# Attention's first two maxima and exponentials ahead of the projection's last rotation

## The reference

```python
q = (x @ Wq + bq).reshape(B, T, H, HD)
k = (x @ Wk + bk).reshape(B, T, HKV, HD)
q, k = _rope(q, cos, sin), _rope(k, cos, sin)
scores = jnp.einsum('bgjtd,bjsd->bgjts', q, k) * scale
scores = jnp.where(mask[None, None, None], scores, -jnp.inf)
wei = jax.nn.softmax(scores, axis=-1)
out = jnp.einsum('bgjts,bjsd->bgjtd', wei, v)
```

## Time and profile before

| what | value |
|---|---|
| time, median of 3 runs | 2125.2 us (2123.72 to 2127.41) |
| the profiled execution: its time | 2124.0 us |
| its span in the trace | 2122.2 us |
| PE busy | 2057.8 us (97% of the span) |
| DVE busy | 1718.2 us (81%) |
| ACT busy | 1370.4 us (65%) |
| mean granted clock of TensorE | 0.989 |

### The profile page before, as it was taken

The page is one execution under the profiler, slowest core; times in us unless marked ns, Lnnn a source line. Parts: engine busy times, 40 slices in busy tenths (PEclk is TensorE's granted clock), DMA queues, the critical chain, the costliest instruction groups (busy, mean ns, idle before and its releaser), DMA issues.

```text
span 2122.2 us, 39177 instructions
## 1 busy us (share of the span) xinstructions
PE 2057.8 (97%) x13409; PEld 1827.4 (86%) x13409; DVE 1718.2 (81%) x3648; ACT 1370.4 (65%) x2752; POOL 851.1 (40%) x818
## 2 busy tenths in 40 slices
PE   8999989999999999999999999999959999999998
PEld 6888878999889998899988999888748999999996
DVE  5899987888678877788767887678877898988887
ACT  3677776766667666676666766433326777777774
POOL 1000013333233332333323333144455777788774
PEclk9999999999999999999999999999979999999999
DMA  7557553110331104311053110567637999999998
GB/s 250 189 213 277 218 213 125 70 60 21 130 120 71 61 21 138 111 70 60 21 203 107 69 62 19 193 239 287 238 122 201 299 298 298 298 297 293 301 287 258
DMA packets 139633, 361.25 MB, mean 170 GB/s; under 512 B 16336, under 2 KB 33232, under 8 KB 134864
## 3 DMA queue, kind: packets, MB, share of 16 engines
q1 hardware_dynamic: 111376, 292.03, 39.2%
q0 software_dynamic: 28096, 67.12, 13.2%
HBM read 224.21 MB, written 134.89 MB: 169 GB/s over the span
## 4 chain that ended last, share of the span: by engine, by line
PE 75%; DVE 5%; ACT 2%; issue 2%; DMA 1%; POOL 0%; DVEq 0%; POOLq 0%; ACTq 0%
PE p_S L665 18%; PE p_O L700 17%; PE p_TP L677 11%; PE p_pgu L1453 9%; PE p_acc L1050 4%; PE p_prest L1453 4%; PE p_py L1470 4%; PE p_tp L1439 3%; PE p_py L1471 1%; PE p_py L1472 1%; DVE p_hi_hot L1237 1%; ACT p_prob L744 1%; DMA o_scratch<-p_oT 1%; ACT p_pT1h L753 0%; PE p_picked L1483 0%
## 5 line engine op out<-in xcount | busy, mean ns | idle before, releaser
L665 PE MATMUL p_S<-p_kT,p_q 128*128 128x512 f32 (+3 forms) x1920 | 474.0, 377 | 12.5 <-ACT p_prob L744 12.0
L665 PEld LDWEIGHTS p_S<-p_kT,p_q 128*128 128x128 f32 x1920 | 323.8, 190 | 63.3 <-ACT p_prob L744 19.2
L859 POOL TENSOR_SCALAR p_prob<-p_prob,p_inv 128x128 f32<-128x128 f32 (+7 forms) x256 | 191.3, 747 | 452.3 <-DVE p_inv L808 452.3
L859 POOL TENSOR_SCALAR p_prob<-p_prob,p_inv,p_part 128x1024 f32<-128x1024 f32 x128 | 153.0, 1195 | 483.4 <-DVE p_inv L813 483.4
L677 PE MATMUL p_TP<-p_ident,p_prob 128*128 128x128 f32 x2176 | 303.5, 274 | 2.4 <-DVE p_pT1l L819 2.1
L677 PEld LDWEIGHTS p_TP<-p_ident,p_prob 128*128 128x128 f32 x2176 | 244.4, 141 | 30.7 <-issue 17.9
L797 DVE TENSOR_REDUCE p_nmax<-p_S 128x1 f32<-128x1024 f32 (+7 forms) x256 | 253.1, 989 | 20.8 <-PE p_S L665 15.5
L753 ACT CAST p_pT0h<-p_TP 128x512 fp32r<-128x512 f32 (+3 forms) x320 | 155.0, 527 | 135.0 <-PE p_TP L677 134.4
L753 ACT CAST p_pT1h<-p_TP 128x512 fp32r<-128x512 f32 (+3 forms) x320 | 154.8, 526 | 128.8 <-PE p_TP L677 128.2
L1723 POOL DMA_INDIRECT sum_scratch<-p_y,p_tokT x124 | 206.0, 1661 | 42.6 <-issue 37.2
L700 PE MATMUL p_O<-p_pT0h,p_v 128*128 128x256 f32 x1088 | 222.8, 288 | 0.0
(11 more groups left out here) (284 smaller groups left out, 4635.0 us busy)
## 6 DMA issues: line engine op xcount, KB each, us to landing
p_w_raw<-in_gu SPq DMA_DIRECT2D x64, 768.0 KB, 6.9
qk_scratch<-p_qout SPq DMA_DIRECT2D x80, 512.0 KB, 2.8
p_q<-qk_scratch SPq DMA_DIRECT2D x16, 2048.0 KB, 9.0
o_scratch<-p_oT SPq DMA_DIRECT2D x128, 256.0 KB, 2.1
p_ot<-o_scratch SPq DMA_DIRECT2D x32, 1024.0 KB, 7.4
p_w_raw<-in_gu SPq DMA_DIRECT2D x64, 256.0 KB, 8.3
v_scratch<-p_vout SPq DMA_DIRECT2D x16, 512.0 KB, 3.2
p_t_raw<-in_dn SPq DMA_DIRECT2D x32, 256.0 KB, 8.2
```

Source lines behind the costliest of these rows:

```text
L665: mm = nc.tensor.matmul(out, x, y, start=(n == 0), stop=(n == 2))
L859: nc.gpsimd.tensor_scalar(prob[k][:, cols], prob[k][:, cols], inv[:, k:k + 1], scale, ALU.mult, ALU.mult).then_inc(normed, 1)
```

## The change

Before the last rotation of the projection, DVE takes the maxima of attention's units 0 and 1, and ACT, right after the swap of block 79, their exponentials. DVE then does rotate(79) and join(79) and enters attend; the low halves of blocks 77, 78 and 79 follow one each at the end of attention's steps 2, 3 and 4. ACT makes the high parts of blocks 77 to 79 after the two exponentials. No instruction is added or taken away; PE, POOL and SP have the programs that they had, and SP's stores of blocks 77 to 79 wait for the same counts.

```diff
-        def scalar(act):
+        def scalar(act, first_exps):
...
                         swap(q, n, k, t, first and k == 0 and t < 2)
+                        if last and k == 1 and t == NT - 1:
+                            first_exps(act)
                         if t >= 2:
                             q_hi_part(q - 2, k, t - 2, i, first)
...
-        def vector(dve):
+        def vector(dve, first_maxima):
...
                     for t in range(NT):
+                        if last and k == 1 and t == NT - 1:
+                            first_maxima(dve)
                         rotate(n * NT + t, n, k, t, first and k == 0)
+                        if last and k == 1 and t == NT - 1:
+                            join(n * NT + t, t, False)
+                            return
                         if t >= 2:
                             q_lo_part(n * NT + (t - 2), k, t - 2)
...
-            for t in (NT - 2, NT - 1):
-                q_lo_part(NH * NT - NT + t, 1, t)
+            return [lambda dve, t=t: q_lo_part(NH * NT - NT + t, 1, t) for t in range(1, NT)]
...
-        FREE = 2
+        FREE, AHEAD = 2, 2
...
-        def steps(eng, step, tail, between={}):
+        def steps(eng, step, tail, between={}, early={}):
             for j in range(HKV):
                 for i in range(U):
                     step(j, i, j == 0)
+                    for piece in early.get((j, i), []):
+                        piece(eng)
...
+            if first_only:
+                for u in range(AHEAD):
+                    exp(0, u, 0)
+                return
...
-                    if i < U and a < ngrp(i):
+                    if i < U and a < ngrp(i) and not (first and i < AHEAD):
                         exp(j, i, a)
...
+            if first_only:
+                for u in range(AHEAD):
+                    row_max(0, u, 0)
+                return
...
-                if i < U:
+                if i < U and not (first and i < AHEAD):
                     row_max(j, i, 0)
...
+                  {(0, AHEAD + n): [piece] for n, piece in enumerate(rest)})
...
-            project.scalar(act)
+            project.scalar(act, lambda act: attend.scalar(act, None, first_only=True))
             attend.scalar(act, early[0])
...
-            project.vector(dve)
-            attend.vector(dve, early[1])
+            rest = project.vector(dve, lambda dve: attend.vector(dve, None, first_only=True))
+            attend.vector(dve, early[1], rest)
```

More of the change, by code:

```diff
@@ L731, in tensor, with scalar @@
             pe.wait_ge(exped, HKV * SG[U])
-        def scalar(act, between):
-            act.sem_inc(weighed, FREE)
+        def scalar(act, between, first_only=False):
+            if not first_only:
+                act.sem_inc(weighed, FREE)
             def exp(j, u, a):
@@ L769, in step, with vector @@
                         p_hi(*args)
-                    if i < U and a < ngrp(i):
+                    if i < U and a < ngrp(i) and not (first and i < AHEAD):
                         exp(j, i, a)
             steps(act, step, OUT - 2, {U + 1: between[0:1], U + 2: between[1:2], U + 3: between[2:4]})
-        def vector(dve, between):
-            dve.sem_inc(turn_lo, FREE)
-            dve.sem_inc(o_lo, FREE)
+        def vector(dve, between, rest=(), first_only=False):
+            if not first_only:
+                dve.sem_inc(turn_lo, FREE)
+                dve.sem_inc(o_lo, FREE)
             def take_k(j):
@@ L847, in step @@
                     p_lo(*args)
-            steps(dve, step, OUT - 2, {U + 2: between[0:1], U + 3: between[1:2], U + 4: between[2:3], OUT - 2 + U: between[3:4]})
+            steps(dve, step, OUT - 2, {U + 2: between[0:1], U + 3: between[1:2], U + 4: between[2:3], OUT - 2 + U: between[3:4]},
+                  {(0, AHEAD + n): [piece] for n, piece in enumerate(rest)})
         def gpsimd(pool):
```

## The result

| what | before | changed |
|---|---|---|
| median, 13 runs each | 2125.2 us (2123.39 to 2128.66) | 2131.22 us (2129.93 to 2135.81) |
| ratio to before | | 1.0028, 95% interval 1.0021 to 1.0035 |
| span of the profiled execution | 2122.2 us | 2128.1 us |

The change makes the kernel 6.0 us slower, by 0.28%; the interval of the ratio is 4.5 to 7.4 us. The forecast was 2128.6, in the right direction, with too small a size; the range ended at 2130.4, 0.8 us short.

What follows compares the result with a forecast made beforehand. The border was taken as bound by low half 79, its store, the load of queries and pair 0's landing behind it. Landing +1.4 and half clock +2.0 us on 2124.0, plus 1.2 to the median, gave 2128.6 us; range 2121.8 to 2130.4.

Steps and rivals of the forecast that it cites:

- What bounds the border: Projection to attention: low half 79, its store, load of queries, pair 0's store landing, then unit 13's scores set the time.
- Maxima and exponentials first: Behind unit 1's scores: PE's gap shrinks from 5.36 to about 1.2 us, 4.2 us earlier for PE alone.
- The low halves' sum: DVE's attend steps up to low half 79 sum to 2.95 us; it ends at 294.9, bounds 294.5 to 295.8.
- The load: SP's load of queries goes out at 297.8, 1.4 us later than before; bounds +1.0 to +2.7.
- it then lands the same 9.7 us after the load's issue: Pair 0's output store, queued behind the load of queries, lands at 307.5, with 1 us allowed either way.
- The range: For the whole kernel's time: 2121.8 to 2130.4 us, with some 0.1 of chance left out on either side.
- the case's own range: The forecast case alone, landing plus clock: 2125.2 + 0 to 2125.2 + 5.6 us; the case had chance 0.46.
- rival 3: Half clock twice, in PE's first stretch and second gap: landing +2.4, second gap 2.9, time 2130.5 us; chance 0.10.
- The clock: Clock falls to half in PE's new gap of some 5 us ahead of unit 13: price 2.0 us, bounds 0 to 2.9.
- Sum: At the border: +1.4 us landing and +2.0 us clock make +3.4 us; forecast 2128.6 us.
- Rivals 1 and 2: 1: clock stays up in PE's gap, 2126.6 us, chance 0.22. 2: pair 0's transfer doesn't bind, 2121.8 us, chance 0.18.
- slower by over 0.2%: Whole kernel slower by more than 4.25 us: chance 0.18, from the half-clock-twice case and the forecast's upper fifth.

Runs made afterwards that it cites:

- after_fill: The changed kernel with PE computing unit 12's scores nine times over, to keep it busy in its gap ahead of unit 13; 2129.73 us.
- after_sp: The changed kernel with SP issuing the stores of pairs 0 and 1 ahead of the wait for the projection's stores and the load of queries; 2127.33 us.
- after_split: The changed kernel with the load of queries in two halves: pair 0's store, wait, first half, pair 1's store, second half; 2125.26 us.
- keys_late: The changed kernel with the load of the keys' third block issued behind pair 3's store instead of pair 1's; 2131.7 us.
- before_split: The kernel before with the load of queries in two halves: wait, first half, stores of pairs 0 and 1, second half; 2126.45 us beside 2126.57.
- lows_only: The changed kernel with only the spread low halves kept; maxima and exponentials of units 0 and 1 back behind the join; 2132.13 us.
- max_only: The changed kernel with only the early maxima and exponentials kept; the three low halves back in their old places; 2127.85 us.
- before_sp: The kernel before with SP's stores of pairs 0 and 1 ahead of the wait and the load of queries; 2128.94 us beside 2125.64.

## Why the prediction was right in kind and short in size

- **What bounds the border**: right. The chain named (low half 79, its store, the load, pair 0's landing, unit 13) is the chain of the changed profile, and after_fill, after_sp and after_split took it apart.
- **Maxima and exponentials first**: right. PE's gap shrank to 1.19 us (1.2 foreseen). Nothing of it reaches the end.
- **The low halves' sum**: "Low half 79 starts at 294.2 and ends at 294.9". Set back by 0.73 us, the later start of attention, it ended at 296.27 - 0.73 = 295.54: within the bounds, 0.6 later than taken. The term missed is DVE's wait of 0.82 us for unit 0's transposed high part, and behind that POOL, whose first scaling took 0.81 us instead of 0.37, and PE's transposes at half clock (0.49 us).
- **The load**: issued at 299.08 - 0.73 = 298.35, +1.9 us; +1.4 was taken. The error is the low half's; from its end to the load it took 2.81 us, where 2.85 was taken.
- **"it then lands the same 9.7 us after the load's issue"**: this is the step that failed. It was 10.4 us in the first trace of the changed kernel and 10.6 in the second. Landing: 309.52 - 0.73 = 308.79, +2.66 us where the sum has +1.4. What differs is how soon the stores of pairs 0 and 1 join the queue behind the load (0.44 and 2.9 us after its issue, for 4.5 and 7.1 before), and the keys' load behind them; the last of these is ruled out by keys_late. The traces speak for pair 0's early store, as above, but it wasn't tried alone, so the cause of these 0.7 to 0.9 us stays open.
- **The range**: it was drawn too narrow by the prediction's own words. They allow the landing 1 us either way, but the 5.6 us of the case's own range are 2.7 for the load's place and 2.9 for the clock, and rival 3, whose time is the upper end, leaves that 1 us out too. With it the own range would have reached 2131.8.
- **The clock**: right, 1.7 us in the first trace and 2.35 in the second, against 2.0.
- **Sum**: +2.66 and +1.8 make 4.45 at the border in the first trace, +2.8 and +2.35 make 5.2 in the second; both end attention 5.2 us behind; the medians are 6.0 apart. With the landing as measured the forecast would have been 2129.9, inside its range. What is left up to 2131.2 has no term in the sum: the traces show it as scatter of the clock's spell and of the stretches outside the border, and the interval of 4.5 to 7.4 us is wide enough for it, but no run shows a cause.
- **Rivals**: what happened is nearest to rival 3 (2130.5), half clock twice: the clock fell in the first stretch too (for 6.8 us in the first trace, with 0.50 over 292 to 294, and for 3.4 us in the second), low half 79 came late, and the landing was +2.66 for its +2.4; only its dearer second gap (2.9) didn't come. Rivals 1 and 2 fell: the clock didn't stay up, and ACT stood 5.6 us for the landing.
- **Chance**: slower by over 0.2% had 0.18, and rival 3 had 0.10. That was too little: the prediction itself has only short matmuls and two gaps between 288.5 and 295, and a falling clock there should have had more weight than one in ten.

## What to carry to other kernels

When a gap of an engine is closed, follow the transfers, not the engine: here the work moved out of the way was what a queue waited for, and the load behind it was ahead of the store that bound everything. The stores issued behind the large load paid for it here: 5.2 and 10.0 us for a store that takes 2.0 alone. Cutting the load in two took the 6 us of loss away (after_split), though on the kernel before it changed nothing (before_split); moving it whole passed a smaller stall two pairs on. And where the bound is a landing, time gained ahead of it became an idle gap of TensorE here, which was paid for once more in half clock.

## What the runs showed of the hardware

**POOL beside DVE.** POOL's scaling of 128x128 took 0.37 us in each of its first four instances before. In the changed kernel:

```profile
295.69 0.83 POOL L880 TENSOR_SCALAR p_prob<-p_prob,p_inv 128x128 f32<-128x128 f32 x1 [1.66 <-DVE p_inv L823]
```

Beside it DVE ran low half 79 from 295.59 to 296.27, and 296.27 + 0.25 is POOL's end: it had all but waited for DVE's end. The low half reads two tensors of SBUF; the transposed low halves read one of theirs from PSUM. The Trainium skill, "SBUF — State Buffer", section "SBUF: two separate sides", says that a DVE operation with two SBUF inputs and a POOL operation that reads SBUF exclude one another for a whole instruction. The rows agree, in both traces of the changed kernel (0.83 and 0.82), in the first scaling there, beside low half 77 (0.81), and in lows_only (0.91 and 0.87); before, beside a transposed low half at 296.22, POOL kept its 0.37. I hadn't weighed it: it speaks against placing SBUF to SBUF subtractions among steps in which PE waits for POOL.

**The clock.** In max_only the granted clock fell to half behind a gap of only 2.02 us (PE at rest from 308.4 to 310.4):

```profile
308.00:310.40 2.40, 0.39 (x5) 0.18 (x3) 1.66 (x5) 1.49 (x5) 0.49 (x1) 1.00 0.41 139
310.40:312.00 1.60, 1.60 (x5) 0.99 (x6) 1.04 (x4) 1.35 (x4) 0.68 (x2) 0.53 0.20 76
312.00:314.00 2.00, 2.00 (x11) 2.00 (x11) 1.51 (x4) 1.16 (x3) 0.69 (x1) 0.52 0.56 137
```

In after_sp it fell for 3.4 us behind the gap of 2.32 us. In before_sp, PE stood 2.44 us ahead of unit 17 (its scores start at 318.92) and the clock stayed up:

```profile
316.00:319.00 3.00, 0.56 (x6) 0.34 (x4) 1.97 (x5) 1.77 (x5) 0.67 (x1) 1.00 0.72 261
319.00:322.00 3.00, 3.00 (x22) 2.73 (x22) 2.45 (x7) 2.23 (x6) 0.71 (x2) 1.00 0.06 14
```

So a gap of two microseconds may or may not cost it. And no gap of that length is needed: in the changed kernel the clock fell at 291.9 (0.98 over 290 to 292, then 0.50), when PE's longest rest since the first scores had been the 1.19 us.
